# Token shift of the second norm by a transfer inside SBUF, and the softmax's three PE stages in a row

## The reference

```python
for i in range(DEPTH):                      # DEPTH = 6
    x = attn_layer(shift_tokens(x), Wqkv[i], q_scale[i], k_scale[i], Wo[i]) + x
    x = ffn_layer(shift_tokens(x), ln_g[i], ln_b[i], W1[i], b1[i], W2[i], b2[i]) + x

def shift_tokens(t):                        # channels 64 to 127 come from the token before
    a, s = jnp.split(t, 2, -1)
    s = jnp.pad(s, ((0, 0), (1, 0), (0, 0)))[:, :-1]
    return jnp.concatenate([a, s], -1)
```

## Time and profile before

| | |
|---|---|
| median of 3 runs | 3447.68 us (3443.36 to 3448.49) |
| the profiled execution | 3448.77 us, span 3446.8 us |
| busy: PE / PEld / DVE / ACT / POOL | 96 / 69 / 85 / 79 / 73% of the span |
| mean granted clock of TensorE | 0.976 of full speed |
| DMA queue of SP | 18.9% of the 16 DMA engines' time |

### The profile page before, as it was taken

One profiled execution on the slowest core, in us unless ns is written; L12 is line 12 of the kernel. 1 busy time (PEld: TensorE's weight loads), 2 busy tenths in 40 slices (PEclk: granted clock), 3 DMA queues, 4 the chain that ended last, 5 costly groups with the idle time before them and its releaser, 6 DMA issues.

```text
span 3446.8 us, 169053 instructions
## 1 busy us (share of the span) xinstructions
PE 3301.8 (96%) x65316; PEld 2378.3 (69%) x65316; DVE 2931.5 (85%) x6259; ACT 2735.7 (79%) x5169; POOL 2502.3 (73%) x2671
## 2 busy tenths in 40 slices
PE   5888789999999999999999999999999999999997
PEld 3444357777777777777777777777777777777775
DVE  6888788888888888888888888888888888888885
ACT  3445588888888888888888888888888888888886
POOL 3333377777778777777778777777778777777774
PEclk9778899999999999999999999999999999999998
DMA  2000021212221211222122211212221112212122
GB/s 75 5 6 5 2 55 49 55 46 55 65 68 46 54 51 49 81 53 55 46 55 62 71 50 50 55 46 75 59 55 47 53 52 68 67 46 55 46 55 54
DMA packets 125539, 175.91 MB, mean 51 GB/s; under 512 B 26742, under 2 KB 49332, under 8 KB 124724
## 3 DMA queue, kind: packets, MB, share of 16 engines
q1 hardware_dynamic: 125492, 175.28, 18.9%
HBM read 21.32 MB, written 2.10 MB: 7 GB/s over the span
## 4 chain that ended last, share of the span: by engine, by line
PE 76%; POOL 9%; issue 7%; DVE 4%; DMA 1%; SPq 1%; ACT 1%; POOLq 0%; DVEq 0%; ACTq 0%
PE bank L1123 16%; PE bank L1233 9%; PE bank L1141 9%; PE bank L1133 8%; PE bank L1204 7%; PE bank L1188 6%; POOL qk L435 4%; POOL qk L444 4%; PE bank L1267 3%; PE bank L1221 3%; PE bank L1275 3%; PE bank L1030 2%; PE bank L1071 2%; PE bank L1242 2%; PE bank L1180 2%
## 5 line engine op out<-in xcount | busy, mean ns | idle before, releaser
L435 POOL TENSOR_TENSOR qk<-ta,tb 128x512 f32<-128x512 f32 x768 | 982.8, 1280 | 11.6 <-DVE tb L855 11.6
L1123 PE MATMUL bank<-wqkv,zsT 128*128 128x512 f32 x1536 | 806.4, 607 | 6.1 <-DVE tb L855 2.4
L444 POOL TENSOR_TENSOR qk<-qk,rn 128x512 f32<-128x512 f32 x768 | 796.0, 1049 | 0.0
L563 ACT ACTIVATE sq<-bank 128x512 f32<-128x512 f32 x768 | 461.0, 600 | 322.9 <-PE bank L1123 313.5
L473 POOL TENSOR_TENSOR P<-P,rowsum 128x512 f32<-128x512 f32 x384 | 401.4, 1046 | 374.7 <-DVE rowsum L971 374.7
L852 DVE TENSOR_TENSOR ta<-bank,rot 128x512 f32<-128x512 f32 x768 | 525.8, 685 | 25.4 <-ACT sq L563 10.0
L855 DVE TENSOR_TENSOR tb<-bank,rot 128x512 f32<-128x512 f32 x768 | 521.2, 679 | 0.0
L956 DVE TENSOR_REDUCE bank<-sq 128x32 f32<-128x2048 f32 x192 | 437.8, 2280 | 0.3
L1133 PE MATMUL bank<-wqkv,zsT 128*128 128x512 f32 x768 | 412.3, 619 | 5.0 <-DVE tb L855 5.0
L1233 PE MATMUL bank<-wo,oT 128*128 128x128 f32 x3072 | 393.9, 281 | 1.4 <-ACT oT L589 1.4
L1233 PEld LDWEIGHTS bank<-wo,oT 128*128 128x128 f32 x3072 | 357.4, 191 | 14.6 <-ACT oT L589 1.8
(11 more groups left out here) (132 smaller groups left out, 6528.8 us busy)
## 6 DMA issues: line engine op xcount, KB each, us to landing
vs<-vt SPq DMA_DIRECT2D x1152, 128.0 KB, 2.4
wqkv<-L_ffn_Wqkv SPq DMA_DIRECT2D x6, 1024.0 KB, 5.1
wqkv<-L_ffn_Wqkv SPq DMA_DIRECT2D x6, 512.0 KB, 3.8
wo<-L_ffn_Wo SPq DMA_DIRECT2D x6, 512.0 KB, 3.7
z_sb<-x SPq DMA_DIRECT2D x4, 512.0 KB, 6.7
ctxb<-ctx SPq DMA_DIRECT2D x32, 64.0 KB, 1.8
out<-x_sb SPq DMA_DIRECT2D x8, 256.0 KB, 3.5
w<-L_ffn_W SPq DMA_DIRECT2D x6, 341.0 KB, 3.1
```

The costliest lines, as they stand in the source:

```text
L435: g.tensor_tensor(o, i0, i1, ALU.add).then_inc(s["g_add"], 1)
L444: g.tensor_tensor(q3, q3, r3, ALU.mult).then_inc(s["g_qk"], 1)
L563: a_.activation(sq[:, 512 * j:512 * j + 512], bank[j % 2][:, :], ACT.Square)\
L1123: t_.matmul(bank[j % 2][:, :], zsT[:, k % 2, :], wqkv[:, 512 * j:512 * j + 512], start=True, stop=True).then_inc(s["p_qk"], 1)
```

## The change

The tile `zm` becomes three parts of 64 channels: part 0 and part 2 are written by `z_mid`, part 1 is the shifted copy of part 2. SP fills it by a transfer inside SBUF of 127 rows of 256 bytes, from partition p to p + 1; partition 0 of part 1 is set to zero once at the start. `norm_stats` and `norm_apply` read parts 0 and 1 in SBUF in place of `bank[6]`, and `norm_stats` waits for the transfer. PE's `shift_tokens` is gone. SP issues one `shift_z` a unit, woven in between the `shift_v` of later units and the weight loads. The orders of the slot change on all engines: on PE `transpose_P`, `scores` and `attend` follow each other (`values_here` becomes a wait in `attend`) and `transpose_z` and `ffn_out` stand ahead of `proj_qk(2)`; on DVE `z_mid` and the four steps of `root` come first, then the statistics, then `z_out`, and `sum_squares` comes ahead of `gated`; ACT and POOL follow. The rotary table is multiplied by 2^8, and the argument of the norms' logarithm and the factor in `root` by 2^16, which cancel; no instruction is added by that.

```diff
-        zm = sb("zm", [128, 2, E])
+        zm = sb("zm", [128, 2, 3, E // 2])
...
+            def shift_z(u, par):
+
+                wait(sp, "d_zm", count(1, u, 1))
+                sp.dma_start(zm[1:128, par, 1, :], zm[0:127, par, 2, :]).then_inc(s[f"l_s{par}"], 16)
+
...
                 with sp.Fori(0, (B - 6) // 2) as i:
                     for k in range(2):
+                        shift_z(i * 2 + (start + k), k)
                         shift_v(i * 2 + (start + 3 + k), (3 + k) % 2)
+                shift_z(end - 6, 0)
                 shift_v(end - 3, 1)
+                shift_z(end - 5, 1)
                 if layer + 1 < DEPTH:
                     load_qk(layer + 1)
                 shift_v(end - 2, 0)
                 if layer + 1 < DEPTH:
                     load_v(layer + 1)
+                shift_z(end - 4, 0)
                 shift_v(end - 1, 1)
+                shift_z(end - 3, 1)
                 if layer + 1 < DEPTH:
                     shift_v(end, 0)
+                shift_z(end - 2, 0)
+                if layer + 1 < DEPTH:
                     shift_v(end + 1, 1)
                     load_o(layer + 1)
+                shift_z(end - 1, 1)
+                if layer + 1 < DEPTH:
                     shift_v(end + 2, 0)
                     load_ffn(layer + 1)
...                                             # POOL's order
                 norm_rstd()
+                add(0)
+                add(1)
+                next_input()
+                normalize(0)
                 residual()
-                add(0)
-                normalize(0)
                 normalize(1)
-                add(1)
                 normalize(2)
-                next_input()
                 normalize(3)
                 add(2)
+                add(3)
                 weigh(0)
-                add(3)
                 weigh(1)
...                                             # ACT's order
+                copy_T(0)
+                copy_T(1)
                 square(0)
-                copy_T(0)
                 log_sum()
-                copy_T(1)
+                square(1)
                 inverse_root()
-                square(1)
                 copy_T(2)
                 copy_T(3)
+                copy_z()
+                copy_PT(0)
+                copy_PT(1)
                 square(2)
                 act.preload_act_table_set("gelu_and_others")
-                copy_z()
-                copy_PT(0)
+                copy_o(0)
                 copy_zn()
                 square(3)
-                copy_PT(1)
                 copy_v(0)
+                copy_o(1)
                 gelu()
                 act.preload_act_table_set("natural_log_exp_and_others")
                 exponent()
-                copy_o(0)
-                copy_o(1)
                 copy_v(1)
...
                     if d_on:
-                        wait(dve, "p_zsh", count(1, d, 1))
-                        v_.bn_stats(stats[:, 0:6], bank[6][:, 0:128]).then_inc(s["d_bn"], 1)
+                        wait(dve, f"l_s{pd}", 16 * (d // 2) + 16 if isinstance(d, int) else (d >> 1) * 16 + 16)
+                        v_.bn_stats(stats[:, 0:6], zm[:, pd, 0:2, :].rearrange("p c e -> p (c e)"))\
+                            .then_inc(s["d_bn"], 1)
...                                             # DVE's order
-                z_out()
+                z_mid()
                 root(0)
-                z_mid()
                 rotary(0)
                 root(1)
+                root(2)
+                root(3)
                 norm_stats()
-                root(2)
                 norm_aggr()
-                root(3)
                 norm_var()
+                z_out()
                 rotary(1)
                 norm_apply()
+                maximum(0)
                 rotary(2)
-                maximum(0)
                 maximum(1)
                 subtract(0)
                 rotary(3)
                 subtract(1)
+                sum_squares()
                 gated()
-                sum_squares()
                 sum_rows()
                 invert()
...
-                def shift_tokens():
-
-                    if d_on:
-                        wait(pe, "d_zm", count(1, d, 1))
-                        wait(pe, "z_ready", (count(1, f, 1) if isinstance(f, int) else d) + B)
-                        t_.matmul(bank[6][:, 0:64], ident, zm[:, pd, 0:64], start=True, stop=True)
-                        t_.matmul(bank[6][:, 64:128], shift, zm[:, pd, 64:128], start=True, stop=True)\
-                            .then_inc(s["p_zsh"], 1)
...                                             # PE's order
                 proj_qk(0)
-                ffn_out()
                 transpose_qk(0)
                 attn_out()
                 proj_qk(1)
                 transpose_qk(1)
-                shift_tokens()
+                transpose_z()
+                ffn_out()
                 proj_qk(2)
-                transpose_z()
                 transpose_P()
                 scores()
+                attend()
                 transpose_zn()
                 proj_qk(3)
-                values_here()
                 proj_v(0)
                 ffn_gate()
                 ffn_a()
-                attend()
                 proj_v(1)
```

More of the change, by code:

```diff
@@ L40 @@
 NORM_MIN2 = 1e-24
+LN_UP = 2.0 ** 16
 MASKED = -(2.0 ** 120)
@@ L65, in constants @@
         c[:, o + 64:o + 128] = np.concatenate([sin * s, -(sin * s)], 1)
+    c[:, C_ROT:C_ROT + 256] *= np.float32(LN_UP ** 0.5)
     q, k = np.arange(WIN)[:, None], np.arange(2 * WIN)[None, :]
@@ L90, in build @@
         ident = cst[:, C_ID:C_ID + 128]
-        shift = cst[:, C_SH:C_SH + 128]
         tri = cst[:, C_TRI:C_TRI + 128]
@@ L185, in build @@
             "l_cst", "l_x", "l_xw", "l_dm", "l_ctx0", "l_ctx1", "l_qks", "l_wqk", "l_wv", "l_wo", "l_w1", "l_w2",
-            "l_gb", "l_b2", "l_rot", "l_v0", "l_v1",
+            "l_gb", "l_b2", "l_rot", "l_v0", "l_v1", "l_s0", "l_s1", "u_s0",
             "u_bf", "u_ones", "u_wkr", "u_rotq", "u_dmT", "u_dmc", "u_ct", "u_ctc", "u_st", "u_ag", "u_ve", "u_rstd",
@@ L339, in _ @@
                     load_ffn(0)
+            sp.wait_ge(s["u_s0"], 1)
             for layer in range(DEPTH):
@@ L374, in _ @@
             g.memset(vaug[:, :, :, :], 0.0).then_inc(s["u_vz"], 1)
+            g.memset(zm[:, :, 1, :], 0.0).then_inc(s["u_s0"], 1)
+            pool.wait_ge(s["u_s0"], 1)
             pool.wait_ge(s["u_vz"], 1)
@@ L458, in residual @@
                         wait(pool, "z_ready", count(1, d - 2, 1) + B if not (isinstance(d, int) and d < 2) else 0)
-                        g.tensor_tensor(zmb[:, pd, :], zm[:, pd, :], b2r[:, :], ALU.add).then_inc(s["g_zmb"], 1)
+                        g.tensor_tensor(zmb[:, pd, :].rearrange("p (c e) -> p c e", c=2), zm[:, pd, 0:3:2, :],
+                                        b2r[:, :].rearrange("p (c e) -> p c e", c=2), ALU.add)\
+                            .then_inc(s["g_zmb"], 1)
                 def next_input():
@@ L627, in log_sum @@
                         wait(act, "a_rn", count(1, m - 1, 1))
-                        a_.activation(lns[:, :], SC[0][:, 0:32], ACT.Ln).then_inc(s["a_ln"], 1)
+                        a_.activation(lns[:, :], SC[0][:, 0:32], ACT.Ln, scale=LN_UP).then_inc(s["a_ln"], 1)
                 def inverse_root():
@@ L867, in root @@
                             wait(dve, "a_rn", count(1, m, 1))
-                            ins = v_.scalar_tensor_tensor(n0, sm, -0.5, ym, ALU.mult, ALU.mult)
+                            ins = v_.scalar_tensor_tensor(n0, sm, -0.5 * LN_UP, ym, ALU.mult, ALU.mult)
                         if i == 2:
@@ L888, in z_mid @@
                         wait(dve, "p_y", count(1, d, 1))
-                        wait(dve, "p_zsh", count(1, d - 2, 1))
                         wait(dve, "g_zmb", count(1, d - 2, 1))
-                        v_.tensor_tensor(zm[:, pd, :], bank[7][:, 384:512], z_sb[:, cols(d)], ALU.add)\
+                        v_.tensor_tensor(zm[:, pd, 0:3:2, :], bank[7][:, 384:512].rearrange("p (c e) -> p c e", c=2),
+                                         z_sb[:, cols(d)].rearrange("p (c e) -> p c e", c=2), ALU.add)\
                             .then_inc(s["d_zm"], 1)
@@ L917, in norm_apply @@
                         wait(dve, "p_znT", count(1, d - 1, 1))
-                        v_.tensor_scalar(zn[:, :], bank[6][:, 0:128], mv[:, 0:1], rstd[:, pd:pd + 1],
+                        v_.tensor_scalar(zn[:, :], zm[:, pd, 0:2, :].rearrange("p c e -> p (c e)"), mv[:, 0:1], rstd[:, pd:pd + 1],
                                          ALU.subtract, ALU.mult).then_inc(s["d_zn"], 1)
@@ L1195, in attend @@
                     if c_on:
-                        pe.wait_ge(s["l_wv"], 16)
+                        wait(pe, f"l_v{pc}", 96 * (c // 2) + 96 if isinstance(c, int) else (c >> 1) * 96 + 96)
                         wait(pe, "a_PT", count(2, c, 2))
+                        pe.nop(nofuse=True)
```

(5 more changed lines are left out.)

2 lines of the change are left out of this document (1 added, 1 removed).

## The result

The changed kernel takes 3678.72 us (3674.99 to 3683.38) against 3448.09 us of the kernel before, run beside it: a ratio of 1.0671, 95% interval 1.0652 to 1.0691. The prediction was 3436; its range ended at 3570. The profiled execution has a span of 3680.3 us.

What follows compares the result with a forecast made beforehand. The prediction took PE to bound the old kernel at 15.48 us a slot and a DVE-and-transfer loop of 15.22 the changed one. Full slots -49, layer ends +29, drain +8 gave -12 us: 3436, range 3325 to 3570.

Steps and rivals of the forecast that it cites:

- the closed loop: From `z_mid` through the transfer and once round DVE to `z_mid`: 11.98 + 3.24 = 15.22 us a slot.
- layer ends: At five layer ends late loads and transfers stall the loop: 6.6 us each, 29 in all after 4 already paid.
- its 1.8 for PE at `load_qk`: At each layer end PE stands 1.8 us for `load_qk`, which lands in 5.1 with 3.1 us left.
- the late `shift_z`: At each layer end `shift_z` comes late, about 1.3 us behind `load_o` and 3.9 behind `load_ffn`.
- the drain: Last slots, where `norm_stats` waits for the transfer: four slots pay up to 2.5 us each, 8 taken in all.
- L: Time from the end of `z_mid` to `norm_stats`: 1.30 fixed, 1.85 rows, 0.09 hand-overs, 3.24 us, from 2.9 to 4.8.
- The fixed part: In the transfer, 0.95 us ahead of the first row and 0.35 behind the last: 1.30, upper end 1.6.
- the first rival: The transfer hides: at 2.1 us or less from `z_mid` to `norm_stats`, PE's 14.7 is the slot, about 3330; chance 0.18.
- DVE's round: DVE's part of the loop, `norm_stats` to the end of `z_mid`: 0.98 + 10.53 + 0.47 = 11.98 us.
- DVE's slack: DVE's waits of 1.02 us before `z_mid` and 0.56 before `z_out`; being late by less costs nothing today.
- No further stall, but no room: ACT and POOL at 15.22 us a slot: 13.1 and 12.2 of work, about 0.4 us left at two points of ACT.
- the second: Slow rows on one engine between `z_mid` and `norm_stats`: at 20 ns a row, slot 15.9 us, 3567 us; chance 0.20.

Runs made afterwards that it cites:

- e12: e1 with two transfers of z at each layer end issued ahead of weight loads: 3468.5 us, 1.0067 to the kernel before.
- e7_112_rows: The changed kernel with only the first 112 of the 127 rows shifted, the last 15 tokens' shifted half left out: 3494.0 us, 1.0131 to the kernel before.
- e1: The changed kernel with the 127 rows sent as two transfers, of 112 and 15 rows: 3489.0 us, 1.0126 to the kernel before.
- e4: The changed kernel with the norm reading the unshifted channels at once, the transfer issued but not waited for: 3480.9 us, 1.0092 to the kernel before.
- e10: e1 with `attend` and `copy_o` back, `rotary(1)` before the statistics, norm and `transpose_zn` later, `square(3)` and layer-end transfers earlier: 3747.0 us, 1.0868 to the kernel before.
- e14: e12 with `rotary(1)` ahead of `norm_stats`, `rotary(2)` of `norm_apply`, `proj_qk(3)` of `attend`, `square(3)` of `copy_o(0)`: 3545.9 us, 1.0281 to the kernel before.
- e15: e12 with `rotary(1)` ahead of `norm_stats` and `rotary(2)` ahead of `norm_apply`: 3615.4 us, 1.0489 to the kernel before.
- e17: e12 with `proj_qk(3)` ahead of `attend`, `square(3)` ahead of `copy_o(0)` and `transpose_P` ahead of `proj_qk(2)`: 3520.3 us, 1.0211 to the kernel before.
- e18: e14 with `transpose_P` ahead of `proj_qk(2)`: 3552.5 us, 1.0303 to the kernel before.
- e9_transfer_only: The kernel before with the shift by one transfer of 127 rows, only DVE's three statistics steps moved behind `root(3)`: 4061.3 us, 1.1776 to the kernel before.
- e6_attend_back: The changed kernel with `attend` behind `ffn_a` again and `copy_o` behind the exponent again: 4017.7 us, 1.1652 to the kernel before.

## Why the prediction was wrong

Right were the mechanism and its form: the closed loop of `z_mid`, transfer and one round of DVE set the slot, PE was no part of it, DVE waits for the DMA of `zm` in each of 192 slots (1.7 us in a full one, predicted 1.0 to 1.1), one engine carries all 127 rows at 14.2 ns (predicted 14.6), and nothing is caught up. Near were the smaller terms: layer ends 5.6 us each (predicted 6.6; its 1.8 for PE at `load_qk` is 2.0 by its own numbers, 5.1 less 3.1), of which the kernel before already had 0.7; the late `shift_z` behind `load_o` and `load_ffn` (e12: 20.5 us for the five, predicted 26); and the drain 9.6 (predicted 8).

Wrong was the length of the loop: 16.49 instead of 15.22. That turned 0.26 us less a slot than before into 1.01 more, and a small gain into a loss. Over 187 slots 1.27 is 237 of the 243 us by which the forecast missed. Two terms were too small, and one statement false.

- **L, 3.24 forecast, 3.72 measured (+0.48).** The rows took 1.8 as forecast. The fixed part didn't. The first bytes come 1.3 us after `z_mid` ends (1.2 in e7_112_rows), not 0.95 and a hand-over; the load of the earlier trace rows, taken as the measure, comes from HBM and has no wait in front, and SP's issue of `zm` takes 0.64 us where the earlier trace rows have 0.34 to 0.53 for one transfer. Behind the last row 0.6 us pass, not 0.35; e7_112_rows, with 16 engines, has the 0.35. So the longer tail goes with the single engine, and why is open. The fit that the first rival took from the Trainium skill, "DMA: Bandwidth & Descriptors", section "Anatomy of one DMA", is given there for transfers that GpSimd issues, and SP issued this one; its 2.1 us are far from the 3.67 measured. The upper end for the fixed part, 1.6, was still below the 1.9 measured.
- **DVE's round, 11.98 forecast, 12.76 measured (+0.78).** By its three pieces, mean of the two turns in the timeline above: `norm_stats` to `rotary(1)` 1.00 (forecast 0.98), `rotary(1)` to the reciprocal 10.92 (10.53), reciprocal to the end of `z_mid` 0.84 (0.47). The forecast moved DVE's operations to other places and kept their spacing. But `sum_squares` behind `subtract(1)` starts 0.81 us after it where `gated` started 0.59 after it; `zn`, read from SBUF, holds the next operation back by 0.54 or 0.36 where it was 0.32; and the stop at the loop's back edge, 0.57 in every other slot (the chain of waits has the loop's own instructions there), now stands ahead of `z_mid`, in the loop. In the kernel before it is the idle time of 0.56 ahead of `z_out`. The prediction read this as slack, while the timeline names no other engine that it waits for: it went with "DVE's slack" into the sum at nothing.
- **"No further stall, but no room".** The walk used the durations of the kernel before and missed that `attend`, between `scores` and `proj_qk(3)`, closes a loop of its own. At 16.49 it doesn't show. With the transfer cut or out of the loop, e1, e4 and e7 stay at 15.4 to 15.5 a slot instead of the 14.7 of the first rival; the chain of e4 shows this loop, that of e7 PE's round. So the rival in which "the transfer hides", 3330 us, was wrong too: with the transfer out of the loop altogether the kernel takes 3481.

The rival that came nearest is the second: slower through the single engine. Its mechanism and its point of decision (a loop longer than today's slot) are right, its cause (20 ns a row) is not: that its 3567 lies nearest to the result is luck; the rows ran at 14.2 and the fixed parts and DVE's own round were long. The range missed, because the bounds were put on L alone: DVE's 11.98 had no upper bound, though the neighbours of its operations changed.

Not settled: why the layer ends, the first and the last slots cost more in the new orders (in e4 27 us, its full slots another 10); and which order of the four engines would use the time that PE no longer has to spend on the shift. Five tries (e10, e14, e15, e17, e18) that were to shorten one loop came out slower; a wait that grew is known for all but e17.

## What to carry to other kernels

Taking work off the engine that is full pays only if what replaces it is not part of a closed loop; before such a change, write down each cycle of dependencies through the slot, with the in-order queues as edges, and compare its length with the slot. Here the transfer's cycle with the cut transfer (15.4), `attend`'s cycle (15.5) and PE's own round (14.8, an estimate) lie within 0.7 us of each other, and a third cycle of 16.5 to 17.9 opens when `attend` goes back, so that each single edit, good by itself, lost to the next one. In such a cycle a transfer counts from the end of the producer to the start of the consumer, every back edge and dependent start counts, and the row count of a transfer matters: 127 rows landed after 3.67 us, 112 after 1.8. And a wait of PE can cost twice: once by itself, and once by the clock that falls behind it (19.5 against 17.8 us a slot in e9_transfer_only).

## What the runs showed of the hardware

- **`zn`, a VectorE operation from SBUF to SBUF, ends with GpSimd's instructions.** 128 x 128, it takes 0.40 to 0.41 us in all 192 cases of the kernel before, where its input is in PSUM. From SBUF it takes 0.43 or 0.62 in the changed kernel, 0.84 to 1.02 in e15_rotary_first, 1.11 to 1.14 in e9_transfer_only and 1.20 to 1.43 in e18_all (5 to 95% of the 192), and in all of these it ends 80 to 89 ns after the end of a GpSimd instruction:

```profile
L940 DVE TENSOR_SCALAR zn<-zm,mv,rstd 128x128 f32<-128x128 f32 x192 | 102.5, 534 | 1.8 <-POOL rstd L469 1.8
...
L942 DVE TENSOR_SCALAR zn<-zm,mv,rstd 128x128 f32<-128x128 f32 x192 | 264.3, 1377 | 1.8 <-POOL rstd L471 1.8
```

(the first line is of the changed kernel, the second of e18_all). It looks as if the operation gets its turn only between two of GpSimd's. The Trainium skill, "SBUF — State Buffer", section "Who interferes with whom", says that such an operation in a two-port mode and GpSimd exclude each other for whole instructions. The trace agrees in the ends 80 to 89 ns apart; no row shows the mode.
- **Too long a loop body.** With four slots in the body instead of two the program loaded 10.16 MB of instructions instead of 0.48 and took 12.8% longer than the changed kernel, at a mean granted clock of 0.92 instead of 0.97 of full speed. The Trainium skill, "Runtime: NRT & Kernel Launch", section "Instruction fetch mechanics", gives PE a store of 2048 instructions; in the changed kernel's trace a slot has 680 instructions of PE and PEld, so two slots are 1360 and four 2720, an estimate that leaves PE's waits and branches out. That it is PE's loop that no longer fits is not shown by these runs, though its stops of 1.6 us in the middle of a stage fit it.
- **A transfer inside SBUF**, from the end of the writing operation to the start of the reading one: 3.72 us for 127 rows of 256 bytes, of which 1.9 are not the rows'.
- **The loop's back edge** shows as 0.57 us in which DVE does nothing, in every second slot, in the kernel before where it cost nothing (0.56) as in the changed one.
- **PE's granted clock** falls from 2.4 to 1.2 GHz for 3.4 us in slots where PE had to wait: 62 of 151 slots of e9_transfer_only (19.3 to 19.5 us instead of 17.8), 53 of 151 of e6_attend_back (19.15 instead of 17.84), none of the same 151 in the changed kernel, where PE waits less.
